# The maxima of four context attentions, split into high and low rows for a one-pass fp32r product

## The reference

```python
q = (xq @ Wq + bq).reshape(B, Lq, nh, dh)
kv = (xkv @ Wkv + bkv).reshape(B, Lkv, 2, nh, dh)
k, v = kv[:, :, 0], kv[:, :, 1]
scores = jnp.einsum('bqhd,bkhd->bhqk', q, k) / jnp.sqrt(jnp.float32(dh))
attn = jax.nn.softmax(scores, axis=-1)
out = jnp.einsum('bhqk,bkhd->bqhd', attn, v)
```

## Time and profile before

| | |
|---|---|
| median of three runs | 1573.97 us (1571.93, 1573.97, 1583.33) |
| the profiled execution | 1573.0 us |
| its span, first to last instruction | 1571.2 us |
| mean granted clock of PE | 0.978 |
| PE busy | 1452.7 us, 92% of the span, 10,495 instructions |
| DVE busy | 1052.8 us, 67%, 2,994 instructions |
| ACT busy | 767.8 us, 49% |
| POOL busy | 395.9 us, 25% |
| chain that ended last | PE 66%, DVE 25%, ACT 4%, issue 2%, DMA 2%, POOL 1% |
| L2140, the reductions of the context attentions | 32 of 1,220 ns, 37.7 us busy |
| L2148, the reciprocals of the context attentions | 16 of 3,356 ns, 53.7 us busy |

### The profile page before, as it was taken

How to read it: one execution, slowest core, us unless ns; L and a number is a source line. 1 busy time by engine, 2 the same in 40 slices (tenths; PEclk the granted TensorE clock), 3 DMA queues, 4 the chain that set the end, 5 groups by cost and what they waited for, 6 DMA issues and landing times.

```text
span 1571.2 us, 26548 instructions
## 1 busy us (share of the span) xinstructions
PE 1452.7 (92%) x10495; PEld 915.3 (58%) x10495; DVE 1052.8 (67%) x2994; ACT 767.8 (49%) x1248; POOL 395.9 (25%) x447
## 2 busy tenths in 40 slices
PE   5889999999999999978998999999999999997898
PEld 3447674344455857656774767444445585765676
DVE  2584356899847446799547544799983754679953
ACT  1335422788844533335552643288884453332554
POOL 4420015642125100113215000664202510001320
PEclk9899998899999999999999999999999999999999
DMA  9500024221020000000040000632102000000000
GB/s 339 174 1 1 0 83 94 42 43 22 2 81 1 1 1 3 2 1 1 1 165 11 1 1 0 165 53 42 22 2 81 1 1 0 3 2 1 1 1 27
DMA packets 41503, 57.86 MB, mean 37 GB/s; under 512 B 10915, under 2 KB 30659, under 8 KB 40603
## 3 DMA queue, kind: packets, MB, share of 16 engines
q1 hardware_dynamic: 25239, 34.71, 6.8%
q0 software_dynamic: 13360, 14.09, 5.1%
q10 hardware_dynamic: 2780, 7.36, 1.3%
HBM read 40.26 MB, written 2.10 MB: 27 GB/s over the span
## 4 chain that ended last, share of the span: by engine, by line
PE 66%; DVE 25%; ACT 4%; issue 2%; DMA 2%; POOL 1%; ACTq 0%; DVEq 0%
PE ps L1039 9%; PE ps L1053 8%; PE ps L488 6%; PE ps L1398 4%; PE ps L898 4%; PE ps L1189 3%; DVE taken L2478 3%; DVE rs L2148 3%; DVE taken L2490 2%; PE ps L876 2%; PE ps L1423 2%; PE ps L1180 2%; PE ps L624 2%; DVE mxw L2140 2%; PE ps L1024 2%
## 5 line engine op out<-in xcount | busy, mean ns | idle before, releaser
L1715 ACT ACTIVATE pt<-ps 128x512 f32<-128x512 f32 x512 | 274.5, 596 | 66.4 <-PE ps L1039 50.7
L2341 DVE TENSOR_REDUCE mm<-ps 128x1 f32<-128x1024 f32 x240 | 288.6, 1222 | 23.3 <-PE ps L1024 20.8
L2596 POOL TENSOR_TENSOR rstd<-ve,minus_half 128x4 f32<-128x4 f32 x32 | 35.0, 1095 | 615.3 <-DVE ve L2012 615.3
L1039 PE MATMUL ps<-qx,kx 50*128 50x512 f32 x512 | 187.8, 457 | 0.8 <-ACT pt L1715 0.8
L1024 PE MATMUL ps<-kx,qx 48*128 48x512 f32 x480 | 180.2, 456 | 1.2 <-DVE mm L2341 1.1
L1053 PE MATMUL ps<-pt,v 128*32 128x256 f32 x2048 | 158.4, 394 | 0.1
L1039 PEld LDWEIGHTS ps<-qx,kx 50*128 50x128 f32 x512 | 79.8, 188 | 88.5 <-ACT pt L1715 69.9
L2225 DVE TENSOR_TENSOR rlo<-ring,rhi 128x512 fp32r<-128x512 f32 x48 | 33.2, 691 | 91.9 <-ACT ring L1667 91.9
L1053 PEld LDWEIGHTS ps<-pt,v 128*32 128x32 f32 x2048 | 44.4, 109 | 84.2 <-ACT pt L1715 56.7
L2643 POOL DMA_DIRECT2D qx<-mxT x64 | 35.9, 563 | 195.7 <-ACT mxT L1709 165.0
L616 PE MATMUL ps<-filler 128*128 128x512 f32 x256 | 83.1, 456 | 0.0
(11 more groups left out here) (378 smaller groups left out, 3380.7 us busy)
## 6 DMA issues: line engine op xcount, KB each, us to landing
wm<-in_L_xcond_W_mlp_dram SPq DMA_DIRECT2D x4, 1024.0 KB, 8.2
w3a<-in_L_xcond_w_m_dram SPq DMA_DIRECT2D x2, 2048.0 KB, 9.0
qx<-q_hi POOLq DMA_DIRECT2D x56, 64.0 KB, 2.3
kx<-k_hi POOLq DMA_DIRECT2D x56, 64.0 KB, 2.3
w<-in_L_xcond_e_w_dram SPq DMA_DIRECT2D x6, 512.0 KB, 7.5
w<-in_L_xcond_e_w_dram SPq DMA_DIRECT2D x2, 1536.0 KB, 13.6
s_ada<-in_L_xcond_w_ada_dram ACTq DMA_DIRECT2D x1, 2304.0 KB, 23.7
w3b<-in_L_xcond_w_m_dram SPq DMA_DIRECT2D x2, 1024.0 KB, 11.3
```

The costliest lines, as they stand in the source:

```text
L1039: pe.matmul(ps[:, bank, :], kx[r, p % 4, kc * P:(kc + 1) * P], qx[r, p % 4, half * 512:(half + 1) * 512], start=True, stop=True).then_inc( ...
L1715: act.activation(pt[:, n % 8, i * 512:(i + 1) * 512], ps[:, bank, :], ACT.Exp, scale=QK_SCALE).then_inc(st_read, 1)
L2341: return dve.tensor_reduce(mm[:, p % 2, e, t:t + 1], place().rearrange("p a q -> p (a q)"), X, ALU.max).then_inc(ring_read, 1)
```

## The change

The reductions write a new fp32 tile `mxt` in place of mxw. After the second one a cast rounds the 32 maxima per partition to fp32r into the first four columns of each group in mxw, and a subtraction writes the rest, maximum less rounded maximum, into the next four. Each of the three steps waits for the one before. After the transposes the high parts lie on rows 32r to 32r+3 of maxT and the low parts on rows 32r+4 to 32r+7; minus_max has a second set of -1 for these, and one product takes off both. maxT and minus_max are fp32r, so the products of L699 take one pass. The window attention keeps its fp32 product, reading minus_max's bits as fp32, and clears the columns of the low parts once per batch, before its first maximum.

```diff
--- before.py
+++ after.py
@@ -153,8 +153,9 @@
         ones_win = keep("ones_win", [P, 2, 32])
         ones_pair = keep("ones_pair", [P, 2 * HD])
         parity = keep("parity", [P, 2])
-        minus_max = keep("minus_max", [P, KC, P])
+        minus_max = keep("minus_max", [P, KC, P], F32R)
         mxw = keep("mxw", [P, T, P])
+        mxt = keep("mxt", [P, 2, 4, 4])
         bk3 = keep("bk3", [P, 2, KC])
         minus_half = keep("minus_half", [P, TB])
         sel_r = keep("sel_r", [P, E, P], F32R)
@@ -248,7 +249,7 @@
         kpair = at("kpair", [P, KC, 2, S], F32, RF + 40 * K1)
         rs2 = at("rs2", [P, 2, BLK], F32, RF + 20 * K1)
         ctxT = at("ctxT", [P, 2, 4, BLK], F32, RF + 24 * K1)
-        maxT = at("maxT", [P, NB, BLK], F32, RF + 42 * K1)
+        maxT = at("maxT", [P, NB, BLK], F32R, RF + 42 * K1)
         m8 = at("m8", [P, 2, H, TOPK], F32, RF + 22 * K1)
         prob = at("prob", [P, 2, 1024], F32, RF + 24 * K1)
         probT = at("probT", [P, 2, HC, P], F32, RF + 32 * K1)
@@ -1273,7 +1274,7 @@
                             pe.matmul(ps[:, 4 + r, odd * P:(odd + 1) * P], kp3[rows, k, odd, c, o:o + P], qT[rows, k, c, o:o + P], start=True, stop=False)
                         for r in range(4):
                             rows = slice(32 * r, 32 * r + 32)
-                            ins = pe.matmul(ps[:, 4 + r, odd * P:(odd + 1) * P], minus_max[rows, c, odd * S:odd * S + 1].broadcast_to([32, P]), maxW[rows, k, o:o + P], start=False, stop=True)
+                            ins = pe.matmul(ps[:, 4 + r, odd * P:(odd + 1) * P], minus_max[rows, c, odd * S:odd * S + 1].bitcast(F32).broadcast_to([32, P]), maxW[rows, k, o:o + P], start=False, stop=True)
                     ins.then_inc(ws_ready, 1)
 
                 def window_values(u):
@@ -2137,9 +2138,11 @@
                         dve.wait_ge(cm_ready, t0 + j + 1)
                         for t in range(2 * j, 2 * j + 2):
                             bank, o = 4 * (j // 2), t % 2 * D
-                            ins = dve.tensor_reduce(mxw[:, t, :].rearrange("p (r n) -> p r n", r=4)[:, :, 0:4],
-                                                    ps[:, bank:bank + 4, o:o + D].rearrange("p r (h s) -> p r h s", s=S), X, ALU.max)
-                        ins.then_inc(cm_read, 1)
+                            ins = dve.tensor_reduce(mxt[:, t % 2, :, :], ps[:, bank:bank + 4, o:o + D].rearrange("p r (h s) -> p r h s", s=S), X, ALU.max)
+                        link(ins)
+                        parts = mxw[:, 2 * j:2 * j + 2, :].rearrange("p t (r n) -> p t r n", r=4)
+                        link(dve.tensor_copy(parts[:, :, :, 0:4].bitcast(F32R), mxt[:, :, :, :]))
+                        dve.tensor_tensor(parts[:, :, :, 4:8].bitcast(F32R), mxt[:, :, :, :], parts[:, :, :, 0:4], ALU.subtract).then_inc(cm_read, 1)
 
                     def divide(u):
 
@@ -2428,6 +2431,8 @@
 
                 def window_maximum(u):
                     t, c = u // KC, u % KC
+                    if u == 0:
+                        dve.memset(mxw[:, :, :].rearrange("p t (r n) -> p t r n", r=4)[:, :, :, 4:8], 0.0)
                     bank = 2 * (u % 2) if u < TB * KC else 0
                     dve.wait_ge(wt_ready, w0 + u + 1)
                     dve.tensor_reduce(mxw[:, t, :].rearrange("p (r n) -> p r n", r=4)[:, :, 2 * c:2 * c + 2],
@@ -2806,6 +2811,7 @@
     for c in range(KC):
         for odd in range(2):
             minus_max[2 * c + odd::32, c, odd] = -1
+            minus_max[4 + 2 * c + odd::32, c, odd] = -1
     minus_max = minus_max.reshape(P, KC, P)
     return {"c_ones_pair": ones_pair, "c_parity": parity, "c_minus_max": minus_max,
             "c_ident": np.eye(P, dtype=np.float32), "c_head_mask": head_mask, "c_ones_ctx": ones_ctx,
```

## The result

| | before | after |
|---|---|---|
| median of 6 runs | 1573.75 us | 1615.21 us |
| lowest, highest | 1571.93, 1584.8 | 1611.02, 1626.69 |
| ratio, 95% interval | | 1.0253 (1.0203 to 1.0302) |
| the profiled execution, its span | 1573.0, 1571.2 | 1626.69, 1624.8 |

The change made the kernel 2.5% slower, 41 us on the medians. Forecast was 1638.6 in a range of 1610 to 1660.

A forecast was written before the change was run, and what follows sets the result against it. The prediction took a ring of DVE and PE to bound the attentions' first half. Attention losses of 58.6 us plus 6 for the clock gave 64.6, so 1637.6 on the profiled execution and 1638.6 on the median, range 1610 to 1660.

The forecast's parts named there:

- ring of DVE and PE: Context attentions, first half: DVE's maxima and PE's scores wait for each other, 3.65 to 4.24 us between maxima ends.
- Rival (2): Attentions: the whole PE saving of 6.9 us comes through and the added pair is hidden, 1567 us; chance 0.02.
- rival (1): Sixteen maxima: the narrow cast and subtraction don't meet POOL and cost only 6.0 us, 1580.0 us; chance 0.09.
- rival (4): Attentions: the first pair waits until POOL's whole run is done, 87 us, with the clock 93, 1667 us; chance 0.05.
- rival (5): Subtracting products: one-pass products don't run side by side, losing 1.6 us in all, 1640 us; counted in the forecast's 0.74.
- The wait for POOL: Maxima beside POOL's weight splits: added cast and subtraction wait for POOL's instructions; attentions lose 58.6 us net, pair costs included.
- Who goes first: DVE against POOL in the attentions: POOL's ready subtraction precedes DVE's subtraction, which then precedes POOL's next instruction.
- rival (3): Attentions: DVE's subtraction gets in before POOL's next instruction; 48.2 us, with the clock 54.2, 1628.2 us; chance 0.10.
- the forecast's order: Each maximum: DVE's cast waits for POOL's running instruction, POOL's next goes in, then DVE's subtraction; 13.1 to 15.3 us an attention.
- The clock: Attentions: PE's longer standstills lower its granted clock, costing 1.5 us an attention, 6 in all, ends 0 and 12.
- The products: Subtracting products on PE, halved by fp32r: 0.39 us an attention won on the path, ends 0 and 0.64.
- costed at nothing: Window clearing, ACT's fp32r copy, minus_max's load, POOL held by DVE, stages after the attentions: no cost counted.

The follow-up runs named there:

- experiment 1: Changed kernel with POOL's split of w1 and w2 held until the four maxima of the first and third attention are read: 1604.1 us, ratio 1.0224.
- experiment 2: Changed kernel keeping the cast and subtraction, but with the product taken as fp32 again: 1628.0 us, ratio 1.0352.
- experiment 3: Changed kernel without cast, subtraction and low part; the reduction writes maxima rounded to fp32r, product one-pass: 1558.7 us, ratio 0.9953 to the kernel before.
- experiment 5: Changed kernel with POOL making both casts of w1 and w2 first, then both subtractions: 1631.4 us in one run.

## Why the prediction was right in its direction, and where it was too high

**What bounds.** Right. Each maximum stands on a ring of DVE and PE, and its lateness shows at full length: 50.5 us at the fourth maxima, 51.3 at the attentions' ends. Rival (2), the pair hidden, is out; rival (1), the pair at 0.2 each beside POOL, is out by the casts of up to 8.07; rival (4), POOL's run uninterrupted, by the casts that end with w1hi and w1lo, in the middle of the run; rival (5), no gain from one-pass products, by the 0.62 a unit.

**The wait for POOL.** Right, and it is the cause: experiment 1 takes POOL away and the wait goes; experiment 2 takes the product away and it stays. Of the 51.3 us, the pairs hold 43.2 (42.1 and the gaps); by the fourth pairs (91.75 to 92.19 in the first attention) they would hold 16 x 0.44 = 7.0 without waits, so some 36 us are waits for POOL. A pair without a wait takes 0.44, near the 0.47 put down.

**Who goes first.** This is the step that failed: "that POOL's next subtraction, which is ready by then, goes before DVE's subtraction". It isn't ready: it waits for its cast to count a semaphore up and starts 0.08 after the cast's end, while DVE's subtraction starts 0.03 after DVE's cast (71.04 against 71.03). So the first pair of the first attention ended at 71.22, not after w1lo, as rival (3) had it (10.9 and 8.9 us against 10.2 and 9.4 measured over the whole attention, for the first and the third). Where POOL's next was a cast, which waits for nothing, it did go first: 1.81 behind w2s's cast, 2.66 behind w2hi's, 3.54 behind w3a's. The first of these stands in the second attention, DVE and POOL:

```profile
466.95 1.81 DVE L2145 TENSOR_TENSOR mxw<-mxt,mxw 128x32 fp32r<-128x32 f32 x1
...
466.83 1.88 POOL L2721 CAST w2s<-wm 128x2048 fp32r<-128x2048 f32 x1
```

The fourth attention has an exception, where POOL's cast came 0.16 us after the instruction before it and DVE's subtraction got in:

```profile
1259.30 0.19 DVE L2145 TENSOR_TENSOR mxw<-mxt,mxw 128x32 fp32r<-128x32 f32 x1
...
1259.38 3.60 POOL L2727 CAST w3a_hi<-w3a 128x4096 fp32r<-128x4096 f32 x1 [0.16 <-issue]
```

So the forecast's order held in the second attention and but for one pair in the fourth, and rival (3)'s in the first pairs of the others, whose second pairs went as the forecast's order has it. Over the whole attention the second and fourth were forecast at 15.1 and measured 14.8 and 16.8, the loss from the clock included. At the maxima the forecast had 4.9 us too much in the first (15.7 for 10.84) and 4.7 in the third (13.5 for 8.85; its own times, 854.2 against the 840.13 at which the maxima ended before, would make 14.1).

**The clock.** Mis-sized: 6 forecast, 10.5 measured, inside the ends given (0 and 12). DVE's idle time before the reductions grew by 7.35, and behind the maxima of the third and fourth attention 3.67 are lost against the 17.32 of the others, 0.53 of which the kernel before lost too. In the second attention, as an example, after:

```profile
466.00:467.00 1.00, 0.00 (x0) 0.90 0.00 0
467.00:468.00 1.00, 0.00 (x0) 0.50 0.00 0
468.00:469.00 1.00, 0.18 (x4) 0.50 0.00 0
469.00:470.00 1.00, 1.00 (x20) 0.50 0.06 16
```

PE stands, the clock falls to the lower level while it stands, and the token scores behind it run at that level. The loss doesn't add to the waits fully: a maximum that comes later for the clock waits the less for the same end of POOL's instruction. In the second attention the pairs came to 12.2 us with their gaps, not 15.5, and only the sum with the clock's part is near the forecast: that agreement is in part luck.

**The products.** Mis-sized by little: 0.39 an attention forecast, 0.60 measured (17.92 to 17.32 in experiments 2 and 3), near the upper end given, 0.64. As forecast, what is won there is DVE's wait for the second sums: the 0.43 of the earlier trace rows is gone.

**The sum.** Maxima's pairs 43.2 for 60.2, clock 10.5 for 6, products 2.4 for 1.6: 51.3 for 64.6, 13 us too much. That is nearer to rival (3)'s 54.2. Of the 17.0 at the pairs some 12 lie in the first and third attention, where the order failed, and some 5 in the second and fourth, where maxima that came later for the clock waited less. The other 10 us of the forecast's error (1638.6 against 1615.2) fit the score loop: the profiled execution of before that the sum was built on had a fall of the clock there, and half of the runs after, by their times, have none: 1573.0 + 51.3 - 11.1 is 1613, beside the three runs at 1611.0 to 1611.6. Which runs without a trace had a fall is inferred. The time came within 5 us of the lower end of the range, which held the forecast and rival (3) alike; that it fell inside says nothing of the order between the engines.

**What was costed at nothing** shows as nothing: the rest of the kernel, outside the attentions and the two score loops, is 0.6 us shorter (0.9 less before the first attention, 0.1 and 0.2 more in the two stretches with the window attention), and POOL's busy time is what it was, 395.7 us against 395.9.

## What to carry to other kernels

Before a small DVE instruction goes on a chain that PE waits for, look at what POOL runs beside it: here a cast or a two-input instruction on SBUF cost the rest of POOL's instruction, up to 8.07 us for 0.18, and sometimes the next one too, while a reduction from SBUF (0.186) and the reductions that read PSUM (2.36) passed. Such a wait is drawn as a long instruction, so compare the least and the greatest duration of one line, and the ends of the two engines. And ask first whether the work is needed: a softmax bears a rounded maximum as long as one number is taken off a whole row, and then the instruction that makes the number can round it for nothing (experiment 3, some 3 us below the kernel before).

## What the runs showed that was not expected

- The turn between DVE and POOL goes by readiness, to a hundredth of a microsecond (71.03 against 71.04): a semaphore wait between two POOL instructions lets a DVE instruction in (0.19), a next one that is free to go doesn't (2.66, and 6.59 in experiment 5).
- The price depends on the phase. POOL's start follows a transfer, so the maxima of the first attention took 22.4 and 25.7 us in two runs with the same DVE and POOL instructions (after, and experiment 2).
- In the attentions the granted clock went to 0.50 nine times after the change, six times while PE stood and three times within 1.3 us after it had resumed. In the score loop it fell for some 27 us in one batch or the other, with PE busy for over 9 of the 10 us before (260 in the kernel before, 1040 after); what starts that stays open.
